# Channel 0 taken off all other channels, its row of x used for weight and bias, and the block's third sum split between ScalarE and GpSimd

## The reference

```python
# layer 0, conv: deformable 3x3 convolution with learned offsets
x = x + einsum("bckhw,ock->bohw", sampled(layernorm(x)), w_conv)
# layer 0, ffn: 8 experts, the best 2 per pixel, n = layernorm(x) over channels
probs = softmax(n @ router_w + router_b)
top_p, top_i = top_k(probs, 2); top_p /= sum(top_p)
x = x + sum_k top_p[k] * (n @ expert_w[top_i[k]] + expert_b[top_i[k]])
# layer 1, conv: channel mixing in the Fourier domain
x = x + real(ifft2(mix(fft2(layernorm(x)), alphas, betas)))
# layer 1, ffn: top-8 rows of each image for each of 64 experts, pooled, a two-layer MLP, scattered back
```

## Time and profile before

| | before |
|---|---|
| median of 3 runs | 3873.42 us |
| the profiled execution | 3877.71 us, its span 3875.7 us |
| PE busy in the span | 3679.2 us (95%) |
| DVE busy | 2944.7 us (76%) |
| ACT busy | 1570.9 us (41%) |
| POOL busy | 1474.4 us (38%) |

### The profile page before, as it was taken

How to read it: one execution, slowest core, us unless ns; L and a number is a source line. 1 busy time by engine, 2 the same in 40 slices (tenths; PEclk the granted TensorE clock), 3 DMA queues, 4 the chain that set the end, 5 groups by cost and what they waited for, 6 DMA issues and landing times. The chain is left out here.

```text
span 3875.7 us, 89814 instructions
## 1 busy us (share of the span) xinstructions
PE 3679.2 (95%) x31511; PEld 2470.7 (64%) x31511; DVE 2944.7 (76%) x9687; ACT 1570.9 (41%) x4565; POOL 1474.4 (38%) x2661
## 2 busy tenths in 40 slices
PE   6999999999999999999979999999999999996667
PEld 5777777777777777777745666666666666654444
DVE  4666666666666666666648999999999999996633
ACT  3444444444444444444411444434343443434224
POOL 4444444444454444444412333333333333333210
PEclk7999999999999999999979999999999999997755
DMA  5655555555555555555527777777777777884789
GB/s 109 108 95 108 100 95 97 96 108 104 91 99 95 108 103 94 96 97 97 88 81 265 270 275 274 272 268 273 277 271 275 267 276 273 285 303 158 268 312 393
DMA packets 611250, 709.81 MB, mean 183 GB/s; under 512 B 62208, under 2 KB 493824, under 8 KB 594416
## 3 DMA queue, kind: packets, MB, share of 16 engines
q1 hardware_dynamic: 505328, 630.10, 58.3%
q10 hardware_dynamic: 104448, 71.85, 6.0%
q0 software_dynamic: 1024, 2.10, 0.2%
HBM read 521.26 MB, written 181.50 MB: 181 GB/s over the span
## 5 line engine op out<-in xcount | busy, mean ns | idle before, releaser
L423 PE MATMUL a_sb<-a_sr,wcv 128*128 128x512 f32 (+3 forms) x2820 | 1052.2, 515 | 0.8 <-DVE a_xo L551 0.8
L405 PEld LDWEIGHTS a_sb<-a_tt,a_win 32*128 32x128 f32 x19008 | 647.0, 186 | 116.3 <-issue 115.5
L423 PEld LDWEIGHTS a_sb<-a_sr,wcv 128*128 128x128 f32 x2820 | 493.1, 190 | 333.9 <-issue 289.1
L405 PE MATMUL a_sb<-a_tt,a_win 32*128 32x144 f32 x19008 | 679.8, 295 | 17.5 <-ACT a_yr L464 11.0
L1171 DVE TENSOR_TENSOR b_P<-b_P,b_x 128x1024 f32<-128x1024 f32 x512 | 620.1, 1212 | 0.0
L509 DVE COPY a_sr<-a_sb 128x432 f32<-128x432 f32 (+14 forms) x1172 | 419.6, 413 | 204.1 <-PE a_sb L405 204.0
L482 ACT COPY a_sr<-a_sb 128x432 f32<-128x432 f32 (+14 forms) x1172 | 362.9, 389 | 356.4 <-PE a_sb L405 356.4
L1074 PE MATMUL b_z<-b_P,b_ew 128*128 128x512 f32 x1024 | 463.4, 596 | 0.0
L1077 PE MATMUL b_z<-b_P,b_ew 128*128 128x512 f32 x1024 | 460.3, 592 | 0.0
L1300 POOL TENSOR_TENSOR b_ss<-b_st 128x12 f32<-128x12 f32 (+2 forms) x139 | 29.9, 215 | 1050.6 <-DVE b_pp L1245 963.5
L545 DVE STREAM_TRANSPOSE a_tt<-a_sx 128x576 f32<-128x576 f32 x520 | 398.7, 768 | 14.2 <-POOL a_sx L576 5.4
(11 more groups left out here) (186 smaller groups left out, 5374.3 us busy)
## 6 DMA issues: line engine op xcount, KB each, us to landing
b_P<-pd SPq DMA_DIRECT2D x128, 2048.0 KB, 7.8
a_win<-xtp SPq DMA_DIRECT2D x2144, 36.0 KB
a_xin<-in_x SPq DMA_DIRECT2D x128, 256.0 KB, 6.0
xtp<-a_tn ACTq DMA_DIRECT2D x128, 256.0 KB, 2.3
x1d<-a_xo SPq DMA_DIRECT2D x128, 256.0 KB, 5.7
b_x<-x1d SPq DMA_DIRECT2D x128, 256.0 KB, 7.7
x2d<-b_xa SPq DMA_DIRECT2D x128, 256.0 KB, 3.5
pw<-x3d SPq DMA_DIRECT2D x128, 256.0 KB, 6.6
```

The costliest lines, as they stand in the source:

```text
L405: t = e.matmul(d[:, 0:3 * m_, :, NU_ * i:NU_ * i + NU_], win[32 * q:32 * q + 32, half_of(Q, j) % NWH, NWIN // 3 * h + i, :], m, start=(j = ...
L423: t = e.matmul(ob[:, r:r + m, :], k["wcv"][:, 3 * (2 - kr) + kx, :], rows[:, :, t_, :], start=(t_ == 0 and r == 0), stop=(t_ == 8))
```

## The change

The row of x for channel 0 gets a double use, and work moves between engines:

- Phase A writes x1 as x_c - x_0 for channels 1 to 127 (channel 0 stays). For that, column 0 of `wcv` is subtracted from the others in setup, and each group gets a new POOL instruction of 128x512 (`level`), which takes the broadcast row of channel 0 (two new DMAs, `load0`) off the input.
- In `read` the identity has a zero at channel 0 and one more column returns x_0 of each pixel.
- `weights` writes only the weights divided by the deviation (32 columns instead of 64). POOL writes the deviation itself (`std_ready`, 128x4) at the end of `scales`. After `read`, a DMA puts the deviation into row 0 of x1. Row 0 of the product then is the plain weight, and row 0 of `ew` is the bias. The ninth product of PE (L1079), its tile `b_pb` and `spread_b` are gone.
- A new POOL stage `clear` zeroes row 0 of x1 (1x512) after the products, ahead of `scales` in POOL's list.
- ACT adds x_0 back when it copies x2 (four activations with a bias in place of one copy).
- `x3` leaves DVE: ACT scales in four activations, POOL adds x2 in one `tensor_tensor` of 128x512, behind `scales` in its list. Its statistics move to a stage `stats3` one slot later, and all that follows is one slot later, so the list has one slot more.
- The loads of phase BC now start after `centred`, with a small DMA of the biases in front of them.

```diff
@@ setup_phase, vector @@
-            e.wait_ge(centred, 1)
+            e.wait_ge(wcv_in, 16)
+            e.tensor_tensor(k["wcv"][:, :, 1:128], k["wcv"][:, :, 1:128],
+                            k["wcv"][:, :, 0:1].to_broadcast([128, 9, 127]), ALU.subtract).then_inc(centred, 1)
+            e.wait_ge(centred, 2)
@@ order_a @@
+        if 0 <= s - 1 < NG:
+            put(t0 + 6, "load0", s - 1)
         if 0 <= s - 2 < NG:
+            put(t0 + 4, "level", s - 2)
@@ phase_a, gpsimd and sync @@
+            elif o[0] == "level":
+                w.wait_ge(x0_in[G % 2], 32 * (G // 2 + 1))
+                w.wait_ge(convolved, 2 * G + 2)
+                e.tensor_tensor(xin[:, G % NX, :], xin[:, G % NX, :], xz[:, G % 2, :], ALU.subtract
+                                ).then_inc(levelled, 1)
+            elif o[0] == "load0":
+                w.wait_ge(levelled, G - 1)
+                for c, n in ((16, 112), (1, 15)):
+                    e.dma_start(xz[c:c + n, G % 2, :],
+                                ins["x"][b * 128, 4 * q * W:4 * q * W + 512].partition_broadcast(n)
+                                ).then_inc(x0_in[G % 2], 16)
@@ STEP @@
-STEP = (("load", -3), ("load2", LAG - 2), ("read", 0), ("turn2", 6), ("fourier", LAG), ("turn3", LAG + 2),
-        ("store2", 6), ("turn_p", 2), ("experts", 4), ("p_out", 2), ("scales", 1), ("best", LAG + 3), ("mixed", 5),
-        ("stats1", 0), ("stats2", 6), ("x3", LAG), ("store3", LAG), ("spread", 2), ("spread_b", 3), ("norm3", LAG + 1),
...
+STEP = (("load", -3), ("load2", LAG - 2), ("read", 0), ("clear", 4), ("turn2", 6), ("fourier", LAG), ("turn3", LAG + 3),
+        ("store2", 6), ("turn_p", 2), ("experts", 4), ("p_out", 2), ("scales", 1), ("best", LAG + 4), ("mixed", 5),
+        ("stats1", 0), ("stats2", 6), ("stats3", LAG + 1), ("x3", LAG), ("store3", LAG + 1), ("spread", 2),
...
@@ phase_bc, tensor @@
             elif stage == "turn_p":
                 w.wait_ge(p_ready, G + 1)
+                w.wait_ge(std_ready, G + 1)
             elif stage == "experts2":
                 for x in range(4, 8):
-                    e.matmul(ZE[u][:, :, :], ew[:, x, :], P[:, G % NPB, :, x, :], start=False, stop=False)
-                w.wait_ge(pb_in[G % NPC], 16 * (G // NPC + 1))
-                e.matmul(ZE[u][:, :, :], ebm[:, :], pb[:, G % NPC, :], start=False, stop=True).then_inc(mixed, 1)
+                    t = e.matmul(ZE[u][:, :, :], ew[:, x, :], P[:, G % NPB, :, x, :], start=False, stop=(x == 7))
+                t.then_inc(mixed, 1)
@@ scalar @@
-                e.copy(xa[:, G % 3], T2[:, :, :]).then_inc(xa_ready, 1)
+                for r in range(4):
+                    t = e.activation(xa[:, G % 3, r, :], T2[:, r, :], ACT.Identity, bias=lr[:, G % NLR, r, 8:9])
+                t.then_inc(xa_ready, 1)
+            elif stage == "x3":
+                w.wait_ge(filtered, G + 1)
...
+                for r in range(4):
+                    t = e.activation(x3t[:, G % 3, r, :], ZC[:, r, :], ACT.Copy, scale=rsr[:, G, 3 - r:4 - r])
+                t.then_inc(x3_scaled, 1)
@@ vector @@
-            elif stage == "x3":
...
-                    t = e.scalar_tensor_tensor(out=x3t[:, G % 3, r, :], in0=ZC[:, r, :],
-                                               scalar=rsr[:, G, 3 - r:4 - r], in1=x2r[:, G % 3, r, :],
-                                               op0=ALU.mult, op1=ALU.add)
+            elif stage == "stats3":
+                w.wait_ge(x3_ready, G + 1)
@@ gpsimd @@
                 e.tensor_tensor(rs[:, u, c], ss[:, u, 2, c], k["mhalf"][:, c], ALU.pow).then_inc(scaled, 1)
+                if G < NG:
+                    w.wait_ge(scaled, G + 1)
+                    w.wait_ge(p_turned, G - 1)
+                    e.tensor_tensor(pp[:, u, 32:36], ss[:, u, 2, 4:8], rs[:, u, 4:8], ALU.mult).then_inc(std_ready, 1)
+            elif stage == "clear":
+                w.wait_ge(z_ready, G + 1)
+                e.memset(x1[0:1, G % NX1], 0.0).then_inc(cleared, 1)
+            elif stage == "x3":
+                w.wait_ge(x2_in[G % 3], 16 * moves(G))
+                w.wait_ge(x3_scaled, G + 1)
+                e.tensor_tensor(x3t[:, G % 3], x3t[:, G % 3], x2r[:, G % 3], ALU.add).then_inc(x3_ready, 1)
@@ sync @@
+        w.wait_ge(centred, 5)
+        e.dma_start(ew[0:1, :, :], ins["eb"][:, :, :]).then_inc(eb_in, 16)
...
+                w.wait_ge(read, G + 1)
+                e.dma_start(x1[0:1, G % NX1], pd[G % NPT * 64 + 32:G % NPT * 64 + 36, :]
+                            ).then_inc(x1_in[G % NX1], 16)
-            elif stage == "spread_b":
```

More of the change, by code:

```diff
@@ L48, in setup_phase @@
     sem = lambda n: ctx.enter_context(nc.semaphore("s_" + n))
-    filled, loaded, w_in, summed, centred = (
-        sem(n) for n in ("filled", "loaded", "w_in", "summed", "centred"))
+    filled, loaded, w_in, summed, centred, wcv_in = (
+        sem(n) for n in ("filled", "loaded", "w_in", "summed", "centred", "wcv_in"))
     T = ctx.enter_context(nc.psum_tensor("s_t", [128, 162], F32))
@@ L284, in phase_a @@
         sem(n) for n in ("rs_step", "z_step", "oc_ready", "hats_ready", "weighed_pool"))
+    levelled = sem("levelled")
     x_in = [sem(f"x_in{i}") for i in range(NX)]
+    x0_in = [sem(f"x0_in{i}") for i in range(2)]
     tn_out = [sem(f"tn_out{i}") for i in range(NTN)]
@@ L487, in vector @@
         e.memset(oc[:, :], 0.0)
+        e.memset(xz[0:1, :, :], 0.0)
         e.memset(sx[:, :, :, :], 0.0)
@@ L759, in _ @@
                 e.memset(bb[:, :], float(3 * PC + 3))
+                e.memset(xz[0:1, :], 0.0)
                 e.wait_ge(started, 16)
@@ L938, in order_b @@
     out = [("load", G) for G in range(3)]
-    for s in range(NG + LAG + 5):
+    for s in range(NG + LAG + 6):
         for stage, lag in STEP:
@@ L1024, in phase_bc @@
     P_in = [sem(f"P_in{i}") for i in range(NPB)]
-    pb_in = [sem(f"pb_in{i}") for i in range(NPC)]
     x2_out = [sem(f"x2_out{i}") for i in range(3)]
@@ L1048, in tensor @@
         w.wait_ge(centred, 5)
+        w.wait_ge(weights_ready, 1)
+        w.wait_ge(eb_in, 16)
         for o in order:
@@ L1059, in tensor @@
                 for r in range(4):
-                    t = e.matmul(RD[:, r // 2, r % 2, 0:136], x1[:, G % NX1, r, :], iw[:, :], start=True, stop=True)
+                    t = e.matmul(RD[:, r // 2, r % 2, 0:137], x1[:, G % NX1, r, :], iw[:, :], start=True, stop=True)
                 t.then_inc(read, 1)
@@ L1113, in scalar @@
                 w.wait_ge(r_step, R_STEPS * (G - 2) + 2)
-                e.copy(lr[:, u].rearrange("p (a b) x -> p a b x", a=2), RD[:, :, :, 128:136]).then_inc(lr_ready, 1)
+                e.copy(lr[:, G % NLR].rearrange("p (a b) x -> p a b x", a=2), RD[:, :, :, 128:137]
+                       ).then_inc(lr_ready, 1)
             elif stage == "weights" and G < NG:
@@ L1138, in scalar @@
             elif stage == "norm3":
-                w.wait_ge(scaled, G + LAG + 1)
+                w.wait_ge(scaled, G + LAG + 2)
                 w.wait_ge(x3_ready, G + 1)
@@ L1183, in vector @@
         e.memset(pp[:, :, :], 0.0)
-        e.memset(pb[:, :, :], 0.0).then_inc(cleared, 1)
         e.memset(st[:, :, :, :], 1.0).then_inc(r_step, 1)
@@ L1187, in vector @@
         w.wait_ge(r_step, 1)
+        e.memset(iw[0:1, 128:136], 0.0).then_inc(weights_ready, 1)
         for stage, G in order:
@@ L1296, in gpsimd @@
                 w.wait_ge(r_step, 1)
-                c = slice(0 if G < NG + 6 else 8, 12 if G >= LAG else 8)
+                c = slice(0 if G < NG + 6 else 8, 12 if G > LAG else 8)
                 sv, dd = ss[:, u, 0, c], ss[:, u, 1, c]
```

107 lines of the change are left out of this document (56 added, 51 removed).

## The result

The kernel after the change takes 3961.41 us (median of 4 runs, 3956.3 to 3962.38); the kernel before, run beside it, 3873.06 us (median of 4, 3870.56 to 3873.45). The ratio is 1.0227, with a 95% interval of 1.0209 to 1.0245: 88 us slower, and 13 us above the predicted 3948.

A forecast was written before the change was run, and what follows sets the result against it. PE was taken to bound the kernel before, and the DVE-POOL loop the kernel after. Terms of 63 + 4 + 3 + 4 + 1 = +75 us on 3873.4 gave 3948 us, range 3845 to 4005.

The forecast's parts named there:

- start of phase BC: At phase BC's start PE's first `read` waits for a load now issued behind `centred`: +3 us, between 0 and 7.5.
- rival A: In phase BC POOL's add of x3 costs DVE nothing: slots 11.59 us, 3860 us; chance 0.26, of which 0.20 faster.
- d: Length of POOL's memset `clear` ahead of `scales` in phase BC, taken as 0.5 us, between 0.19 and 0.74.
- What bounds the kernel before: In steady slots of phase BC PE is the bound at 11.79 us, with DVE full too.
- The loop of 11.35 behind them: In phase BC `scales` waits for `p_ready` and `weights` for `scaled`; this DVE-POOL chain takes 11.35 us per slot.
- `clear` adds 0.24 us: In phase BC POOL's memset ahead of `scales` lengthens the loop of DVE and POOL by 0.24 us per slot.
- The add's wait: In `weights` POOL's add of x3 holds up DVE's subtraction after the maxima by 0.75 us, bounds 0 and 1.08.
- `std` waits for the first product: In phase BC POOL's `std` sits out DVE's first product in `weights`, to about 1.4 us after the power.
- ACT, SP and PE's clock: In phase BC ACT's extra instructions (at most 2.7 us) and SP's DMAs cost 0; PE's clock falls, chance 0.02.
- Phase A, 0: `level` adds 1.08 us to POOL where it waits 4.3 us for DVE, plus two DMAs per group: cost 0.
- rival C: In phase A `level` waits for channel 0's broadcast or blocks DVE: 0.3 us per group, +38 us; chance 0.06.
- Rival B: In phase BC the loop doesn't bind and PE's 10.93 us per slot rules: 3786 us; chance 0.04.

The follow-up runs named there:

- both reliefs: The kernel before without PE's ninth product and with DVE's product of x3 cut to one of 4 columns: 3820.97 us, ratio 0.9868.

## Why the prediction was right, and where it wasn't

The direction, the place and most of the size were right: a loop between DVE and POOL, lengthened by the add's collision with DVE in `weights`. Step by step, against the 84.9 us of the two spans:

| step | predicted | measured |
|---|---|---|
| 116 slots of the steady length | +64 (12.34) | +73.3 (12.41) |
| the slots before them | +3 | +0.9 |
| start of phase BC | +3 | +4.0 |
| end of phase BC | +4 | +4.1 |
| setup | +1 | +1.6 |
| phase A | 0 | +2.4 |
| phase DE | 0 | -1.4 |

(Of the prediction's 63 + 4, one of the two slots that go from 11.36 to 12.34 is counted in the first line and the other in the second, as measured. One side sum of the prediction is slightly off: rival A with d = 0.74 comes to 3891 and not 3888.)

- **What bounds the kernel before: wrong.** The prediction read PE as the bound at 11.79, because PE was busy 400 of 400. It was DVE, at 392 of 400, which in that window waits for nothing. Taking away PE's product alone gave a ratio of 0.9995. A DVE that is busy 98% is a full one: 391.8 of 400 in that run, 391.8 with the loop opened, 391.5 with the add on DVE. The working by which "DVE's sum" was 11.53 left out the small gaps between its instructions. It did no harm, since the change relieves both engines and the forecast went by the loop.
- **The loop of 11.35 behind them: right.** 11.37 with both reliefs, 11.32 with the change and a short add (there L1296 has half its columns).
- **`clear` adds 0.24 us: wrong.** Its length was right (0.51 us recorded, 0.5 taken), the gap ahead of it was not: 0.05 us in place of 0.25. It ends just when `p_ready` would have let `scales` go, and moving it away gave nothing back.
- **The add's wait: right in kind, too small.** 0.75 us was taken, from the order L1208, add, subtraction. The row shows the order that gives the upper end: POOL's add, already standing, gets in ahead of L1259, and the wait is 1.08 us (1257 ns against 179). So 11.32 + 1.09 = 12.41 stands where 11.59 + 0.75 = 12.34 was worked out. Two errors, of +0.27 and -0.34, nearly cancel, and that the forecast lies only 13 us off is luck to that extent: with `clear` priced right and the rest as it stood, it would have been some 31 us lower.
- **`std` waits for the first product: wrong.** It starts 0.08 us after the power, at 2650.77, before the product, and takes 0.21 us. This is the step behind the one above: because `std` doesn't wait, the add is issued during the first product, stands there, and goes ahead of L1259.
- **ACT, SP and PE's clock: right.** POOL waited for ACT's x3 8.3 us in all (128 groups), and the granted clock in the window is 1.00 in both kernels.
- **Phase A, 0: right.** In the two traces its last output comes 2.4 us later than setup explains, but that is scatter. From the first memset of `a_oc` to the end of the last store of x1, the eight traces with the old phase A take 1979.4 to 1985.6 us, mean 1981.8, and the five with the new one 1980.4 to 1983.2, mean 1981.8. `level` lasts 1.27 us and not 1.08, and POOL waits in it for channel 0's broadcast 10 times, 39.4 us in all, as rival C feared. None of it lengthened phase A beyond that scatter.
- **Start of phase BC: right in kind.** PE's first `read` waits 5.12 us for the load of x1, as this row of the timeline of the kernel after shows; the loads are issued at 2009.88.

```profile
2009.88 2.72 SPq L1378 DMA_DIRECT2D b_x<-x1d  x6
...
2012.71 0.57 PE L1097 MATMUL b_rd<-b_iw,b_x 128*128 128x137 f32 x1 [5.12 <-DMA b_x<-x1d]
```

Rival A, the add for nothing, is what the cut add shows: slots 11.32 and 3828 us, lower than its 3860 because `clear` too is free. Its premise fell: DVE is stopped by POOL. Rival B's 3786 for a loop that doesn't bind came true only where the loop was opened by hand (3775). The kernels with the unused add and with the memsets separate the mechanism from all else in the change: reading on POOL costs 100 us, writing for the same time 0.

The Trainium skill's page "SBUF — State Buffer", section "SBUF: two separate sides", describes an exclusive lock. The prediction's estimate from it was 0.72 to 1.08 us, and the measured 1.08 is its upper end. The lock is borne out in both directions (L1259 at 1257 ns, L1341 at 1186), and so is its limit to POOL instructions that read SBUF (the memsets). That the lock is held for the whole instruction is not: DVE's product ran at 1.19 us within POOL's power.

## What to carry to other kernels

Work moved to an engine that is nearly idle isn't free for the one it leaves: ask which instructions it will lie beside, and whether DVE reads two operands from SBUF there while the other reads any. Put it beside work that reads PSUM or one operand; here the same add cost 133 us at the start of `weights` and held up no instruction of DVE behind it. And where one engine is at 100% and another at 98%, take both as full: relieve one alone and count on nothing; look for the loops that stand behind them before adding up the saving.

## What the runs showed of the hardware

- Of the two engines that both want to read, it isn't the next in time that wins but the one already standing: POOL's add, held since 2650.93 by a DVE product, ran before the DVE instruction that followed the product directly. That makes an add of 1.12 us cost DVE its whole length in every slot.
- Four columns on POOL can cost POOL 1.18 us when a DVE product of 1.22 us is under way (with 512 columns it is 2.24), and the same four columns cost DVE nothing.
- The small `std` of POOL and DVE's L1253 meet as well, and both go through: 0.21 us, and 192 ns in place of 174.
- POOL's power of 12 columns stands behind a DVE product (3.32 us in place of 2.27), but a DVE product that starts within it keeps its 1.19 us. The length of a POOL instruction isn't what it costs DVE.
- POOL began the memset 0.05 us after the DVE product that released it, and `scales` 0.25 us after the L1245 that released it. `scales` has one more wait (`z_ready`) behind the one for `p_ready`, `clear` has none; whether that makes the difference stays open.
